# Two hops of a graph network: PSUM banks, row buffers and the order of picks, sums and compares

## What is computed

```
head_emb, tail_emb, rel_emb = e[head], e[tail], relation_emb[relation_type]
ricci = l2_normalize(tail_emb + rel_emb)
hyper_head = expmap0(head_emb)
hyper_tail, hyper_rel = expmap(tail_emb, hyper_head), expmap(rel_emb, hyper_head)
res = project(mobius_add(hyper_tail, hyper_rel))
res = relu(logmap(res, hyper_head) + ricci * 1e-07)
e = l2_normalize(sums_over_head(res) / counts)      # twice
```

## Time and profile before

| | |
|---|---|
| median of 3 runs | 23745.33 us (23739.36 to 23776.59) |
| the profiled execution | 23831.74 us, its span 23829.8 us |
| mean granted TensorE clock | 0.621 |
| PE busy | 10305.7 us, 43% |
| DVE busy | 15503.2 us, 65% |
| ACT busy | 2726.6 us, 11% |
| POOL busy | 12726.1 us, 53% |

### The profile page before, as it was taken

How to read it: one execution, slowest core, us unless ns; L and a number is a source line. 1 busy time by engine, 2 the same in 40 slices (tenths; PEclk the granted TensorE clock), 3 DMA queues, 4 the chain that set the end, 5 groups by cost and what they waited for, 6 DMA issues and landing times. The chain is left out here.

```text
span 23829.8 us, 208218 instructions
## 1 busy us (share of the span) xinstructions
PE 10305.7 (43%) x47565; PEld 6803.8 (29%) x47566; DVE 15503.2 (65%) x25810; ACT 2726.6 (11%) x6634; POOL 12726.1 (53%) x12678
## 2 busy tenths in 40 slices
PE   0033335655555555556666522221433433333333
PEld 0033332222222222222222322221333333333333
DVE  8744439998888888886666211112666666666677
ACT  0011110000000000000000000000222222222222
POOL 0188876666556565536666166663544442544543
PEclk9999995555555555558888555555555555555555
DMA  4033331111111111121111111114222222222222
GB/s 171 23 69 69 69 65 26 24 24 21 23 23 23 21 23 23 23 20 24 24 24 24 7 21 21 21 21 44 54 56 51 54 56 48 52 56 51 57 51 47
DMA packets 1151512, 957.51 MB, mean 40 GB/s; under 512 B 803964, under 2 KB 920316, under 8 KB 1150740
## 3 DMA queue, kind: packets, MB, share of 16 engines
q0 software_dynamic: 419904, 437.84, 11.2%
q1 hardware_dynamic: 730960, 512.22, 8.4%
HBM read 734.68 MB, written 210.63 MB: 40 GB/s over the span
## 5 line engine op out<-in xcount | busy, mean ns | idle before, releaser
L1451 POOL DMA_INDIRECT tail<-ball,h_idx x3328 | 3396.5, 1021 | 3961.9 <-DVEq L1761 1514.0
L737 PE MATMUL p_rad<-w_stack,hid_t 99*128 99x512 bf16 (+1 forms) x6656 | 3077.4, 619 | 2396.3 <-DVEq L827 1117.3
L809 DVE TENSOR_REDUCE red<-prod 128x96 f32<-128x1536 f32 x1664 | 2901.3, 1744 | 3.5
L1487 PE MATMUL h_sum<-head,h_hot 128*128 128x64 f32 x6656 | 1468.1, 422 | 3078.8 <-ACT head L1529 2472.1
L1101 POOL DMA_INDIRECT l_xg<-h_tab,l_idx x1664 | 1573.9, 946 | 1470.0 <-issue 958.3
L1487 PEld LDWEIGHTS h_sum<-head,h_hot 128*128 128x128 f32 x6656 | 1435.4, 332 | 3109.7 <-issue 3109.7
L338 POOL DMA_INDIRECT rec_a<-rec,slot x1600 | 1990.0, 1244 | 517.1 <-issue 510.1
L693 POOL DMA_INDIRECT rec_b<-l_rcb x1600 | 1926.1, 1204 | 570.9 <-issue 514.6
L932 POOL DMA_INDIRECT l_xg<-x_tab,l_idx x1664 | 1574.1, 946 | 1156.7 <-issue 856.8
L948 PE MATMUL l_sum<-outer,l_hot 128*128 128x512 f32 x3328 | 1671.6, 666 | 986.6 <-DVEq L993 904.8
L737 PEld LDWEIGHTS p_rad<-w_stack,hid_t 99*128 99x128 bf16 (+1 forms) x6656 | 773.4, 132 | 4338.8 <-issue 4335.4
(11 more groups left out here) (368 smaller groups left out, 18688.7 us busy)
## 6 DMA issues: line engine op xcount, KB each, us to landing
hot_t<-rows_l SPq DMA_DIRECT2D x208, 512.0 KB
rec_a<-fill SPq DMA_DIRECT2D x128, 728.0 KB, 19.5
l_rec<-rec_a SPq DMA_DIRECT2D x104, 896.0 KB, 4.8
rhot_t<-rows_r SPq DMA_DIRECT2D x208, 384.0 KB
tail<-ball,h_idx POOLq DMA_INDIRECT x3328
t<-in_type SPq DMA_DIRECT2D x100, 500.0 KB
l_xg<-in_x,l_idx POOLq DMA_INDIRECT x1664
l_xg<-x_tab,l_idx POOLq DMA_INDIRECT x1664
```

What stands on the lines that cost most here:

```text
L737: ins = pe.matmul(p_rad[j % 2][:, h * 512:(h + 1) * 512], hid_t[j // 4 % 2][0:K3 + 3 * (1 - i), j % 4, i, :], w_stack[i][0:K3 + 3 * (1 - i ...
L809: ch.step(dve.tensor_reduce(red[:, j, :], prod[j % 3][:, :, :], AX, ALU.add))
L1451: pool.indirect_dma_start(tg[q][:, j, :], None, table[:, :], bass.IndirectOffsetOnAxis(ap=idx[q][:, j:j + 1], axis=0)).then_inc(gathered[q ...
L1487: ins = pe.matmul(p_sum[:, j // 2, :], hot[j // HP8 % 2][:, j % HP8, :], hg[:, j, 0:D], start=(j % 2 == 0), stop=(j % 2 == 1))
```

## The change

- **PSUM.** `p_sum` shrinks from the block's four banks to two of one unit each; the heads get three banks, the relations two.
- **Row buffers.** `hot_t` and `rhot_t` get a third buffer. Units 0 and 3 share buffer 0, unit 1 has buffer 1, unit 2 buffer 2. The room comes from `v2`, DVE's scratch for products, which now lies in `hot[0]`.
- **Rows.** SP loads units 1, 2 and 0 of block b + 2 as the picks of block b + 1 leave their buffers, and unit 3 of block b + 1 once that block's first four quads are picked.
- **Picks.** Of block b + 1 the quads 0 and 1 stand behind the sums of unit 0 of block b, 2 and 3 behind those of unit 1, 4 and 5 behind unit 2, and the other ten behind unit 3. The first waits for three compares at once. The heads of quad k wait for the copy of quad k - 3, its relations for that of k - 2.
- **ACT.** Its copies are dealt in the same way behind the Relus of units 1, 2 and 3.
- **Sums and adds.** The sums of unit u wait for the adds of unit u - 2. DVE's adds of units 0 and 1 stand in the unit loop, behind the `hots` of units 2 and 3.
- **Compares.** Units 1 and 2 stand where 0 and 1 stood, unit 0 in the wait for the logarithm, unit 3 ahead of the adds of unit 2.

```diff
-AHEAD = 8
+AHEAD = 16
...
-        hot_t = [sb(f"hot_t{k}" + tag, [P, BT, P], BF16) for k in range(2)]
-        rhot_t = [sb(f"rhot_t{k}" + tag, [3 * NREL3, BT, P], BF16) for k in range(2)]
-        v2 = sb("v2" + tag, [P, BT, D])
+        hot_t = [sb(f"hot_t{k}" + tag, [P, BT, P], BF16) for k in range(3)]
+        rhot_t = [sb(f"rhot_t{k}" + tag, [3 * NREL3, BT, P], BF16) for k in range(3)]
+        v2 = hot[0][:, :, :].rearrange("p t (a d) -> p (t a) d", d=D)
         sc = sb("sc" + tag, [P, 38, W])
-        p_head = [ps(f"h_head{k}" + tag, [P, 4, P]) for k in range(2)]
-        p_rel = ps("h_rel" + tag, [P, 4, P])
-        p_sum = ps("h_sum" + tag, [P, N2, D])
+        p_head = [ps(f"h_head{k}" + tag, [P, 4, P]) for k in range(3)]
+        p_rel = [ps(f"h_rel{k}" + tag, [P, 4, P]) for k in range(2)]
+        p_sum = [ps(f"h_sum{k}" + tag, [P, BG, D]) for k in range(2)]
...
             def rows(b, u):
-                h = u % 2
-                hold(sp, turn, picked, (b * HU + u) * H + (AHEAD - H))
+                h = u % 3
+                hold(sp, turn, picked, b * Q + AHEAD + (0, H * 2 - Q, H * 3 - Q, H)[u])
...
             def body(b, q, it, left):
-                rows(b, 0)
-                rows(b, 1)
+                if left == 2:
+                    hold(sp, turn, tails_read, b + 2)
+                    lists(b + 2, q)
                 if left:
-                    hold(sp, turn, tails_read, b + 1)
-                    lists(b + 1, 1 - q)
-                    hold(sp, turn, ends_used, b + 1)
-                    edge_ends(b + 1, 1 - q)
-                rows(b, 2)
-                rows(b, 3)
-
-            lists(0, 0)
-            edge_ends(0, 0)
+                    rows(b + 1, 3)
+                if left == 2:
+                    rows(b + 2, 1)
+                    hold(sp, turn, ends_used, b + 2)
+                    edge_ends(b + 2, q)
+                    rows(b + 2, 2)
+                    rows(b + 2, 0)
+
+            for b in range(2):
+                lists(b, b)
+                edge_ends(b, b)
+                for u in (1, 2, 0):
+                    rows(b, u)
+                if b == 0:
+                    rows(0, 3)
...
-            def pick(b, chunk):
-                for k in range(Q):
-                    u, i = k // H, k % H
-                    if i == 0:
-                        hold(pe, turn, hot_done, b * HU + (u + 1))
-                    hold(pe, turn, taken, b * Q + (k + 1))
-                    for j in range(4):
-                        for part in range(3):
-                            pe.matmul(p_head[k % 2][:, j, 0:T_PICK], hot_t[u % 2][:, 4 * i + j, :],
-                                      parts[:, bass.ds(chunk[2 * k + j // 2], 1), part, :], start=(part == 0), stop=(part == 2))
-                    hold(pe, turn, rel_taken, b * Q + (k + 1))
-                    for j in range(4):
-                        ins = pe.matmul(p_rel[:, j, 0:D + 2], rhot_t[u % 2][:, 4 * i + j, :], rel_parts[:, :], start=True, stop=True)
-                    ins.then_inc(picked, 1)
+                return chunks(pe, g["map"][1], b * (N2 // PACK) + u)
+
+            def pick(b, k, chunk):
+                u, i = k // H, k % H
+                if k == 0 or k == 3 * H:
+                    hold(pe, turn, hot_done, b * HU + (3 if k == 0 else 4))
+                hold(pe, turn, taken, b * Q + (max(0, k - 2) + 1))
+                for j in range(4):
+                    for part in range(3):
+                        pe.matmul(p_head[k % 3][:, j, 0:T_PICK], hot_t[u % 3][:, 4 * i + j, :],
+                                  parts[:, bass.ds(chunk[k // 2][2 * (k % 2) + j // 2], 1), part, :], start=(part == 0), stop=(part == 2))
+                hold(pe, turn, rel_taken, b * Q + (k + 1))
+                for j in range(4):
+                    ins = pe.matmul(p_rel[k % 2][:, j, 0:D + 2], rhot_t[u % 3][:, 4 * i + j, :], rel_parts[:, :], start=True, stop=True)
+                ins.then_inc(picked, 1)
 
             def body(b, q, it, left):
-                hold(pe, turn, added, b + 1)
-                chunk = []
-                for j in range(W):
-                    if j % BT == 0:
-                        if left:
-                            chunk.extend(words(b + 1, j // BT))
-                        hold(pe, turn, relu_done, b * HU + (j // BT + 1))
-                    if j % HP8 == 0:
-                        hold(pe, turn, edge_hot, b * (2 * HU) + (j // HP8 + 1))
-                    ins = pe.matmul(p_sum[:, j // 2, :], hot[j // HP8 % 2][:, j % HP8, :], hg[:, j, 0:D], start=(j % 2 == 0), stop=(j % 2 == 1))
-                    if j % HP8 == HP8 - 1:
-                        ins.then_inc(sum_done, 1)
-                if left:
-                    pick(b + 1, chunk)
+                chunk = {}
+                for u in range(HU):
+                    if left:
+                        for w in (u, u + HU):
+                            chunk[w] = words(b + 1, w)
+                    hold(pe, turn, added, b * HU + (u + 1))
+                    hold(pe, turn, relu_done, b * HU + (u + 1))
+                    for j in range(u * BT, u * BT + BT):
+                        if j % HP8 == 0:
+                            hold(pe, turn, edge_hot, b * (2 * HU) + (j // HP8 + 1))
+                        ins = pe.matmul(p_sum[u % 2][:, j % BT // 2, :], hot[j // HP8 % 2][:, j % HP8, :], hg[:, j, 0:D],
+                                        start=(j % 2 == 0), stop=(j % 2 == 1))
+                        if j % HP8 == HP8 - 1:
+                            ins.then_inc(sum_done, 1)
+                    if left:
+                        for k in range(2 * u, 2 * u + 2 if u < HU - 1 else Q):
+                            pick(b + 1, k, chunk)
...
-            def quads(b):
-                for k in range(Q):
+            def quads(b, which):
+                for k in which:
                     hold(act, turn, picked, b * Q + (k + 1 + AHEAD))
-                    act.activation(rg[:, 4 * k:4 * k + 4, :], p_rel[:, :, 0:D + 2], ACT.Copy).then_inc(rel_taken, 1)
-                    act.activation(hg[:, 4 * k:4 * k + 4, :], p_head[k % 2][:, :, 0:T_PICK], ACT.Copy).then_inc(taken, 1)
+                    act.activation(rg[:, 4 * k:4 * k + 4, :], p_rel[k % 2][:, :, 0:D + 2], ACT.Copy).then_inc(rel_taken, 1)
+                    act.activation(hg[:, 4 * k:4 * k + 4, :], p_head[k % 3][:, :, 0:T_PICK], ACT.Copy).then_inc(taken, 1)
...
                 relations(0)
+                relations(1)
                 for u in range(HU):
-                    if u < HU - 1:
-                        relations(u + 1)
                     z = slice(u * BT, u * BT + BT)
                     hold(act, turn, asked, b * (5 + HU) + (6 + u))
                     act.activation(hg[:, z, 0:D], hg[:, z, 0:D], ACT.Relu).then_inc(relu_done, 1)
+                    if u == 0:
+                        relations(2)
+                    elif left:
+                        quads(b + 1, range(2 * u - 2, 2 * u))
+                    if u == 1:
+                        relations(3)
                 if left:
-                    quads(b + 1)
+                    quads(b + 1, range(2 * HU - 2, Q))
...
+                h = u % 3
+                dve.wait_ge(rows_in[h], (b * 2 + (u // 3 + 1)) * 32 if h == 0 else (b + 1) * 32)
...
                 if left:
-                    compares(b + 1, 0)
                     compares(b + 1, 1)
+                    compares(b + 1, 2)
...
                 op(lambda S, S2, E, B2, z: tt(S(26), S(26), E(T_S), MUL_))
+                if left:
+                    compares(b + 1, 0)
                 dve.wait_ge(told, b * 4 + 4)
...
+                def add_unit(u):
+
+                    dve.wait_ge(sum_done, b * (2 * HU) + (2 * u + 2))
+                    add_groups(dve, ch, chunk[u * BG:u * BG + BG], acc, lambda k: p_sum[u % 2][:, k:k + 1, :])
+                    dve.sem_inc(added, 1)
 
                 for u in range(HU):
                     z = unit(u)
...
                     dve.sem_inc(asked, 1)
                     for m in range(2):
                         hots(q, b, 2 * u + m)
+                    if u >= 2:
+                        add_unit(u - 2)
                 dve.sem_inc(ends_used, 1)
-                for u in range(HU):
-                    dve.wait_ge(sum_done, b * (2 * HU) + (2 * u + 2))
-                    add_groups(dve, ch, chunk[u * BG:u * BG + BG], acc, lambda k: p_sum[:, u * BG + k:u * BG + k + 1, :])
-                dve.sem_inc(added, 1)
                 if left:
-                    compares(b + 1, 2)
+                    compares(b + 1, 3)
+                add_unit(2)
+                add_unit(3)
+                if left:
                     tails(1 - q, it + q)
-                    compares(b + 1, 3)
                     heads(1 - q, b + 1)
...
```

25 lines of the change are left out of this document (12 added, 13 removed).

## The result

The changed kernel takes 23183.7 us (median of 4 runs, 23173.2 to 23200.0), the kernel before beside it 23744.3 (4 runs). The ratio is 0.976, with a 95% interval of 0.9745 to 0.9779: 561 us less, where 639 were forecast. On a chip where PE's signals come on time it is not so, which the experiments show.

The account below looks back on a forecast made before the run. Bound: DVE waiting 27 us a block for rows and picks. Shown block: 23.0 gone, 12.2 new, 1.7 from order and rounding; mean 13; 50 x 13 - 10 = 640 us less, 23105 us, range 22750 to 23530.

Parts of the forecast that it names:

- Rows on time: DVE's idle time ahead of the compares falls from 20.9 us a block to under 2.
- The ring: Two sum banks make sums wait for adds of two units earlier: 12.2 us of new waits in the shown block.
- The ten quads: PE's ten quads behind the last sums take about 2.2 us each, leaving no wait ahead of the heads.
- rival A: Picks keep their pace of 3.1 us a quad: gain 4 us a block, 23555 us; chance 0.12.
- Together: The mean block gets 13 us shorter; 50 x 13 - 10 = 640 us less in all.
- old waits: DVE's waits for rows and picks: 27 us in the mean block, 23.0 in the shown block, where all go.
- order and rounding: 1.7 us of the shown block's 12.5 us gain, from the order of compares and adds and from rounding.
- POOL: POOL's idle time per block falls from 31 us to under 20; its work needs 103 us a block.
- Rival C: POOL becomes the bound, its batches growing from 12.9 to 16 us: gain 6 us a block, 23445; 0.08 with another rival.
- The premise: PE's signals are seen late while POOL issues gathers, 4.9 us at one copy; taken as a property, reason unknown.
- Rival B: Sums, adds and halves of units 2 and 3 decide; signals 8 us late at each turn: slower, 23855 us; chance 0.08.

Follow-up runs that it names:

- third chip: Both kernels rerun unchanged on a chip with no remote waits: before 22407.9 us, changed 22462.6 us, ratio 1.0025.
- The last run: The changed kernel with only one gather in eight, on the fifth chip: 22501.3 us beside a kernel before of 23409.2 us.
- first chip: The chip of the first measurement of both kernels: before 23744.3 us, changed 23183.7 us, ratio 0.976.
- fifth chip: The chip of the changed kernel with one gather in eight: 22501.3 us, the kernel before 23409.2 us.
- The third buffer alone: The kernel before with only the third row buffer and the compares' new places: 22183.0 us, ratio 0.990; again on the third chip 22179.4 us, 0.9895.
- the slow picks: Each quad's twelve head matmuls issued three times: kernel before 22648.0 us (1.010), changed 22808.0 (1.017), the third buffer alone 22446.0 (1.001).
- the adds early: The changed kernel with DVE's adds of a unit one unit earlier: 22420.1 us, ratio 1.000 to the kernel before.

## Why the prediction was right, by its steps

*Rows on time.* Forecast under 2 us ahead of the compares, measured 0.9 instead of 20.9. This step carries the gain: 20.0 us a block here, 4.8 on the third chip.

*The ring.* Forecast 12.2 us of new waits in the shown block, 7.6 of them ahead of the halves. The shown block kept its timetable to 2 us. In the mean block halves and adds wait 7.4 us more than before (17.1 against 9.7), so this term was 4.8 too dear. Most of it doesn't depend on late signals, as 5.8 us are there without any. Nor is all of it the ring's: by the variant with three sum banks the dealt picks, whose place ahead of the sums I priced only at unit 1, hold up the sums by themselves.

*The ten quads.* Forecast 2.2 us each and no wait ahead of the heads; they took 2.7 in the shown block, and the mean wait is 4.2 instead of under 3. This step failed, about halfway to rival A. The 2.2 was read off a few copies of before whose remote waits were 2.3 us at most; in the block of after ACT waits 7.2, 3.4 and 5.1 us remotely within these quads, and PE itself strings the matmuls of two of them out.

*Together.* The forecast took 23.5 us of old waits as gone, and 21.8 went (20.0 ahead of the compares, 1.8 ahead of the heads). It credited 1.7 to order and rounding; instead 2.0 were lost in smaller gaps. These 5.4 us too much of gain and the 4.8 too much of cost nearly cancelled, and 13 became 12.4. The total was partly right by luck. The 79 us by which the time was missed have another source in the main: I took 86 us off since the profiled execution of before stood that far above its median, but that of after stands 9 below its own. It took 23174.7 us where 23192 was reckoned.

*POOL.* Its wait was to fall from 31 us a block to under 20; it is 421.7 / 21 = 20.1, just short of that. Rival C doesn't hold. By the Trainium skill (SBUF — State Buffer, section "SBUF: two separate sides") POOL's descriptors wait while DVE holds the shared ports. The traces don't show a price for it that matters: one gather took 1035 ns in after where DVE is busier, 1025 in before, and no block was bound by it.

*The premise.* I took the late signals as "a property of PE's signals while gathers are being issued". The last run bears out that the gathers have a part: in the hops the late signals go with them. That run took away the gathers' traffic with their issue, so which of the two delays the signals isn't separated. And gathers aren't enough. On the first chip POOL issues 1292 of them in before from 11000 to 13000 us, 646 a millisecond, and 1320 from 17000 to 19800, 471 a millisecond; yet no wait from 11000 to 16000 is put down to "remote". The second and third layer, from the first gather of L932 to the last of L1101, take 5637 us there, 5636 on the fifth chip and 5622 on the third, while the first layer's gathers (L671), where signals are late, span 6892, 6693 and 6542. What is needed besides gathers isn't shown. What the prediction didn't say is that the lateness isn't everywhere: three of five chips show no remote wait at all. Each chip was measured in one stretch of time, so whether it belongs to the chip or to its state then isn't separated either. The block can be written as two terms:

| us a block | before | after | gained |
|---|---|---|---|
| signals on time (third chip) | 113.6 | 114.3 | -0.7 |
| added on the first chip | 20.9 | 7.8 | 13.1 |
| first chip | 134.5 | 122.1 | 12.4 |

The whole gain is in the second row. The two rows come from different chips, so that is a difference and not an experiment of its own. Rival B, slower by the ring, is what happens where that row is empty: its price was named rightly (waits between sums, adds and halves), but its condition the wrong way round. I had it decide where signals are later than 3 us; it decides where they are never late, because the waits that the change removes are then 4.8 us and no longer cover it.

*Open.* The third buffer alone was never run where signals are late, so which part of the change is worth how much there isn't separated. It would save the 7.4 us ahead of halves and adds, but its sixteen quads stand behind all sums, and with the slow picks it lost 5.0 us a block at 1.8 us a quad. At the 2.7 to 3.1 us of the first chip it can lose more, so it may be the better kernel there or the worse one. Nor is it known why some chips see PE's signals late.

## What to carry to other kernels

When a profile shows a wait "remote", price the change twice, with the lateness and without it: a gain that lives on it can vanish on the next chip. Take apart a change of several parts before keeping it: here one part (a third row buffer) paid 1% and the rest (four sum banks made two, with the adds in the loop) cost 1.3%, both on a chip without late signals. Two banks put the consumer's adds into the producer's path, and dealt picks put other work there; the adds early bought 1.1 us of the 5.4 back, a third sum bank 0.5. When one cost seems free on top of another, run it without the other: here the two banks and the dealt picks each hid what the other costs.

## What the runs showed of the hardware that I had not expected

- The same kernel took 22408, 22417, 22432, 23409 and 23744 us on five chips. The two slow ones are those whose traces hold remote waits behind PE; before the hops they are slower too: the tanh just ahead of the hops (L1308), up to which all these kernels are the same, comes at 16442 to 16486 us on the first chip, 16283 on the fifth, and 16112 to 16130 on the three others.
- It isn't the picks alone, whose table address comes from a register (`bass.ds(chunk...)`): the matmuls of the first layer (L737) have constant addresses, and DVE waits there for late signals in the trace of after:

```profile
DVE prod L800 <- remote: 279.1, 74, 4.6
ACT hid_t L713 <- remote: 249.9, 9, 29.2
```

- Letting POOL run up to sixteen gathers ahead in a block instead of eight removed landing waits of 285 us in 17 blocks and shortened no block, only the two first blocks.
